# Cross attention: three rotating two-bank units in PSUM, one side bank, and one reduction for two maxima

## The reference, cut to what matters

```
q = split_heads(layernorm(x) @ w_q.T + b_q)      # (4, 16, 256, 16)
k = split_heads(ctx @ w_k.T + b_k)               # (4, 16, 4096, 16)
v = split_heads(ctx @ w_v.T + b_v)
weights = softmax(einsum('bhqd,bhkd->bhqk', q, k) / 4)
x = x + merge_heads(einsum('bhqk,bhkd->bhqd', weights, v)) @ w_o.T + b_o
```

## Time and profile before

| what | us |
|---|---|
| median of 3 runs | 4542.27 (4541.48 to 4546.44) |
| span of the profiled execution (its own time is not given apart from this) | 4533.8 |
| first cross attention: first maximum to last reduction of a maximum | 41.3 to 1019.2 |
| second: first maximum to last reduction of a maximum | 3071.3 to 4037.3 |
| TensorE, VectorE, ScalarE busy over the span | 4131.4, 3154.7, 2854.8 |

### The profile page before, as it was taken

The page is one execution under the profiler, slowest core; times in us unless marked ns, Lnnn a source line. Parts: engine busy times, 40 slices in busy tenths (PEclk is TensorE's granted clock), DMA queues, the critical chain, the costliest instruction groups (busy, mean ns, idle before and its releaser), DMA issues. The chain is left out here.

```text
span 4533.8 us, 83813 instructions
## 1 busy us (share of the span) xinstructions
PE 4131.4 (91%) x30832; PEld 2952.2 (65%) x30832; DVE 3154.7 (70%) x7414; ACT 2854.8 (63%) x5769; POOL 1819.9 (40%) x1862
## 2 busy tenths in 40 slices
PE   6999999988988999999999999977999999986898
PEld 4555555555757788887888878864555555544787
DVE  5677777776777667666676676645677777767645
ACT  3666666667866776767767777733666666664322
POOL 3222222213557555555555555523222222201544
PEclk8999999999999999999999999998999999998999
DMA  6655655535020001011010111017556655522265
GB/s 152 137 108 101 111 99 110 95 62 209 1 75 5 26 21 44 15 38 33 27 33 14 37 33 34 16 37 141 118 103 113 113 107 109 91 45 69 79 177 187
DMA packets 208206, 354.18 MB, mean 78 GB/s; under 512 B 26927, under 2 KB 110564, under 8 KB 205745
## 3 DMA queue, kind: packets, MB, share of 16 engines
q1 hardware_dynamic: 200217, 338.42, 33.5%
q0 software_dynamic: 7584, 10.39, 0.7%
HBM read 257.48 MB, written 114.98 MB: 82 GB/s over the span
## 5 line engine op out<-in xcount | busy, mean ns | idle before, releaser
L757 DVE TENSOR_REDUCE xa_m_part<-xa_ring 128x1 f32<-128x512 f32 x2048 | 1319.2, 686 | 503.5 <-PE xa_ring L910 489.0
L679 ACT ACTIVATE xa_ex<-xa_sc 128x1024 f32<-128x1024 f32 x1024 | 991.6, 1022 | 124.4 <-PE xa_sc L896 109.7
L910 PE MATMUL xa_ring<-xa_ks,xa_q_base 48*128 48x512 f32 x2048 | 521.5, 500 | 169.7 <-DVE xa_m_part L757 130.1
L1077 POOL TENSOR_SCALAR lt_p<-lt_p,lt_stat 128x192 f32<-128x192 f32 x384 | 360.4, 939 | 507.4 <-DVE lt_stat L1067 507.1
L924 PE MATMUL xa_pv<-xa_ex,xa_vs 128*17 128x256 f32 x8192 | 553.4, 388 | 1.1 <-issue 1.1
L910 PEld LDWEIGHTS xa_ring<-xa_ks,xa_q_base 48*128 48x128 f32 x2048 | 202.7, 186 | 500.4 <-DVE xa_m_part L757 431.8
L1090 ACT ACTIVATE lt_p<-lt_bank,lt_stat,lt_rq 128x128 f32<-128x128 f32 (+1 forms) x768 | 365.7, 480 | 218.9 <-DVE lt_stat L1060 214.5
L1929 PE MATMUL lt_bank<-lt_wp,lt_xt 128*128 128x512 f32 x1728 | 461.9, 409 | 16.0 <-DVE lt_wp L1766 7.1
L896 PE MATMUL xa_sc<-xa_q_base,xa_ks 50*128 50x256 f32 x4096 | 424.5, 303 | 27.7 <-ACT xa_k L659 4.1
L896 PEld LDWEIGHTS xa_sc<-xa_q_base,xa_ks 50*128 50x128 f32 x4096 | 349.4, 189 | 121.2 <-ACT xa_vs L666 24.4
L1929 PEld LDWEIGHTS lt_bank<-lt_wp,lt_xt 128*128 128x128 f32 x1728 | 314.6, 192 | 79.3 <-DVE lt_xt L1759 8.4
(11 more groups left out here) (332 smaller groups left out, 8166.4 us busy)
## 6 DMA issues: line engine op xcount, KB each, us to landing
xa_ks<-keys SPq DMA_DIRECT2D x372, 256.0 KB
keys<-xa_kp SPq DMA_DIRECT2D x128, 512.0 KB, 3.8
xa_cx<-in_ctx_t SPq DMA_DIRECT2D x64, 512.0 KB
lt_u<-in_lt_wqkv SPq DMA_DIRECT2D x54, 256.0 KB
places<-in_moe_blank SPq DMA_DIRECT2D x47, 258.0 KB, 8.7
moe_xs<-places SPq DMA_DIRECT2D x47, 258.0 KB
lt_w<-in_lt_w SPq DMA_DIRECT2D x6, 1536.0 KB
xa_q_base<-xa_m_rows SPq DMA_DIRECT2D x512, 2.0 KB
```

What stands on the lines that cost most here:

```text
L679: act.activation(x.ex[:, n % x.NE, :, :], x.sc[n % 2][:, :, :], ACT.Exp).then_inc(*x.ex_done.one())
L757: dve.tensor_reduce(x.m_part[:, i % 2, qt, h, ch:ch + 1], x.bank(n + odd), AX.X, ALU.max).then_inc(*x.dve_out.one())
L910: pe.matmul(x.bank(n + odd), x.q_base[rows, pair, b * S + qt * P:b * S + (qt + 1) * P], x.ks[unit % x.NU][rows, pair % 4, ch * 512:(ch + 1 ...
L1077: pool.tensor_scalar(sv, sv, self.stat[:, n % 5, 3, 1:2], None, ALU.mult).then_inc(*self.div_pool.one())
```

## The change: what it does

- PSUM is divided anew: three units of two banks, one bank for `pv`, one bank called `side`.
- Maxima and scores take the units in turn (S, M, S, M, ...). With three units a use waits for the use three before, which is always of the other kind: S(n) waits for R(n-2), and M(n) for E(n-1).
- The two heads of a maximum fill the two banks of a unit and signal once; one reduction makes two maxima (128x2 out of 128x1024 where there were two of 128x1 out of 128x512).
- All side work of the main loop has the one side bank, so each side step waits until the one before it has been taken away. Before the first maximum, key and query projections rotate through the side bank and the two banks of the last unit.
- The order within a turn is S, M, W, W, S, M, then `place_max`, then side work. Jobs move from 0 and 4 to 2 and 6; `max_rows` stays at 0 and `gather` at 4. Queries, `turn_out` and `project_out` keep their turns, which are at 2 and 6 of a quad as well, and stand behind the job.
- The wait of the first maxima for the turned input (`xt_dve`, `xt_act`) moves from the side step to the maximum.

```diff
-            self.ring = [ps(f"ring{i}", [P, 512]) for i in range(self.NW)]
-            self.pv = ps("pv", [P, S])
-            self.sc = [ps(f"sc{i}", [P, 4, S]) for i in range(2)]
+            self.units = [ps(f"unit{i}", [P, 2, 512]) for i in range(self.UNITS)]
+            self.pv, self.side = ps("pv", [P, 512]), ps("side", [P, 512])
...
-            if t < 0 or at % 4 == 0:
+            if at in (2, 6) or t < 0:
                 job = next(jobs, None)
...
-            scores = [("scores", n) for n in (t, t + 1) if 0 <= n < total]
-            first, second = ([("max", top)], [("max", top + 1)]) if top < total else ([], [])
-            out += first + side + second + scores if side else first + scores + second
-            if second and top % 8 == 6:
+            for odd in range(2):
+                if 0 <= t + odd < total:
+                    out.append(("scores", t + odd))
+                if top < total:
+                    out.append(("max", top + odd))
+                if odd == 0:
+                    out += [("weigh", n) for n in (t - 2, t - 1) if 0 <= n < total]
+            if top < total and top % 8 == 6:
                 out.append(("place_max", top // 8))
-            for n in (t - 2, t - 1):
-                if 0 <= n < total:
-                    out.append(("weigh", n))
+            out += side
...
+        first = [("side", self.side)] + [(f"{n}", self.units[2][:, n, :]) for n in range(2)]
...
+            if kind in ("max", "scores"):
+                n = unit % self.UNITS
+                names, place = [f"{2 * n - 4}", f"{2 * n - 3}"], self.units[n]
+                unit += 1
+            elif kind in ("key", "query") and not started:
+                name, place = first[early % 3]
+                names, early = [name], early + 1
+            elif kind in ("key", "value", "query", "gather", "max_rows", "turn_out", "project_out"):
+                names, place = ["side"], self.side
...
+            self.place_of[step] = place
+            self.before[step] = [done[n] for n in names if n in done]
+            for n in names:
+                done[n] = self.away[step]
...
-                for odd in range(2):
-                    on.wait_ge(x.full, n + odd + 1)
-                    h = 2 * pair + odd
-                    dve.tensor_reduce(x.m_part[:, i % 2, qt, h, ch:ch + 1], x.bank(n + odd), AX.X,
-                                      ALU.max).then_inc(*x.dve_out.one())
+                on.wait_ge(x.full, n + 1)
+                dve.tensor_reduce(x.m_part[:, i % 2, qt, 2 * pair:2 * pair + 2, ch:ch + 1],
+                                  x.place_of[step][:, :, :], AX.X, ALU.max).then_inc(*x.dve_out.one())
...
-            if step in x.use:
-                n = x.use[step]
-                bank = x.bank(n)
-                for m in ((n, n + 1) if kind == "max" else (n,)):
-                    if x.before[m] is not None:
-                        on.wait_ge(*x.before[m])
-            if step in x.exps:
-                on.wait_ge(x.ex_done, x.exps[step])
-                on.wait_ge(x.xt_dve, NT // 4)
-                on.wait_ge(x.xt_act, NT // 4)
+            if step in x.place_of:
+                bank = x.place_of[step]
+                for gone in x.before[step]:
+                    on.wait_ge(*gone)
```

More of the change, by code:

```diff
@@ L316, in __init__ @@
             "p (w k n) -> p w k n", w=2, k=KC)
-        self.banks = [self.sc[i // 2][:, 2 * (i % 2):2 * (i % 2) + 2, :].rearrange("p j s -> p (j s)")
-                      for i in range(4)]
+        self.banks = [self.units[i // 2][:, i % 2, :] for i in range(4)]
         f, d = c.flow, c.dma_flow
@@ L386, in steps @@
                             side.append(("ctx", m + 2))
+            if at == 0 and 0 <= quad + 1 < 4 * self.ITEMS:
+                side.append(("max_rows", quad + 1))
+            if at == 4 and 1 <= quad <= 4 * self.ITEMS:
+                side.append(("gather", quad - 1))
             b, at_b = divmod(t - 10, 12)
@@ L415, in count_uses @@
     def count_uses(self):
-        self.use, self.bank_of, self.away, self.before = {}, [], [], []
-        self.exps, self.cleared, self.chunk = {}, {}, {}
+        self.use, self.place_of, self.away, self.before, self.chunk = {}, {}, {}, {}, {}
         count = {"dve": 0, "act": 0}
-        last, ring, side, done = {}, 0, 0, [0, 0]
+        done, unit, side, early = {}, 0, 0, 0
         started = False
+        first = [("side", self.side)] + [(f"{n}", self.units[2][:, n, :]) for n in range(2)]
         for step in self.plan:
@@ L427, in count_uses @@
             started = started or kind == "max"
[L428 to L431, removed]
             if kind in ("key", "query"):
                 self.chunk[step] = len(self.chunk)
-            if kind not in ("key", "value", "query", "max", "gather", "max_rows", "turn_out", "project_out"):
-                continue
-            self.use[step] = len(self.away)
@@ L437, in count_uses @@
[L437 to L446, removed]
-                count[engine] += 1
[L448 to L451, removed]
@@ new lines, in count_uses @@
+            if kind != "scores":
+                engine = "dve" if kind in ("max", "project_out") else "act"
+                count[engine] += 1
+                self.away[step] = (self.dve_out if engine == "dve" else self.act_out, count[engine])
+                self.use[step] = len(self.use)
+            else:
+                self.away[step] = (self.ex_done, step[1] + 1)
+            self.place_of[step] = place
+            self.before[step] = [done[n] for n in names if n in done]
+            for n in names:
+                done[n] = self.away[step]
@@ L564, in sp @@
                 b = i // x.NKB
-                on.wait_ge(*x.away[x.use[step]])
+                on.wait_ge(*x.away[step])
                 if i:
@@ L629, in act @@
             if step in x.use and kind not in ("max", "project_out"):
-                n = x.use[step]
-                bank = x.bank(n)
+                n, bank = x.use[step], x.place_of[step]
             if kind == "weights":
@@ L909, in pe @@
                     rows = slice(64 * odd, 64 * odd + x.ROWS)
-                    pe.matmul(x.bank(n + odd),
-                              x.q_base[rows, pair, b * S + qt * P:b * S + (qt + 1) * P],
-                              x.ks[unit % x.NU][rows, pair % 4, ch * 512:(ch + 1) * 512],
-                              start=True, stop=True).then_inc(*x.full.one())
+                    mm = pe.matmul(bank[:, odd, :],
+                                   x.q_base[rows, pair, b * S + qt * P:b * S + (qt + 1) * P],
+                                   x.ks[unit % x.NU][rows, pair % 4, ch * 512:(ch + 1) * 512],
+                                   start=True, stop=True)
+                mm.then_inc(*x.full.one())
             elif kind == "weigh":
@@ L919, in pe @@
                 on.wait_ge(x.pv_zero, 1)
-                on.wait_ge(*x.away[x.use["value", i, kt // 2]])
+                on.wait_ge(*x.away["value", i, kt // 2])
                 if kt == 0:
@@ L953, in pe @@
                 b, = a
-                on.wait_ge(*x.away[x.use["turn_out", b]])
+                on.wait_ge(*x.away["turn_out", b])
                 on.wait_ge(x.late_in, 2 if x.ins["bv"] is None else 3)
```

31 lines of the change are left out of this document (14 added, 17 removed).

## The result

The changed kernel takes **4648.28 us** (median of 4 runs, 4636.82 to 4653.14) where the kernel before took 4541.88 beside it (4540.15 to 4546.44): ratio **1.0228, 95% interval 1.0212 to 1.0244**. It is slower by 106 us. The forecast was 4494, faster.

A forecast was written before the change was run, and what follows sets the result against it. TensorE was taken to set the pace, losing waits of about 0.3 us. Per cross attention 42 + 6 - 11 - 18 + 5 = 24 less, 48 in both: 4542.3 - 48 = 4494 us, 8-in-10 range 4400 to 4545.

The forecast's parts named there:

- The failed step: Main loop: SP's row copies move to a turn's end, keys come one turn later of six or so: 0.
- The reduction: VectorE's double reduction of 1024 elements takes 1.19 us; worth nothing by itself, as VectorE doesn't set the pace.
- The rule on smaller instructions: Skill's advice against the double reduction: by it TensorE waits up to 0.5 more, eight times, 4 us a quad.
- The plain quad: Main loop quad without combine: 13.78 in place of 14.50, 0.72 less; 42 us less in a cross attention.
- Combine: Five quads with combine steps: 8 in place of 10.1 over plain ones, three times; 6 less per cross attention.
- The exponential in the last block: A batch's last block: ScalarE's exponential waits for VectorE; 1.15 each, 16 times, 18 more per cross attention.
- The start: Before the main loop: 1.0 less in each of 9 jobs, taken as 5 less per cross attention.
- Rival 3: Main loop: TensorE's pauses for ScalarE drop the clock; slower, 4616 at one quad in 12; chance 0.06.
- Rival 2: Main loop: E late by 0.15 more each turn, 0.6 of 0.72 a quad lost; 4540 or so; chance 0.09.
- The tests that I set: Forecast wrong if a plain quad stays above 14.3, S waits for R, or mid-stretch clock falls below 0.95.

The follow-up runs named there:

- Experiment 1: Also written e1: the changed kernel with SP's load of a unit's keys (`stack_k`) ahead of the turn's side work; 4501.43 us, ratio 0.9988 to the kernel before.
- 2: The kernel before with `stack_k` one turn later, where a job stands in front of it in SP's queue; 4595.33 us, ratio 1.0210.
- experiment 4: Also written e4: Experiment 1's kernel with two reductions of 512 in a unit in place of one of 1024; 4503.78 us, ratio 0.9995 to the kernel before.
- experiment 7: Experiment 1's kernel with the exponential between blocks two turns later, behind the copy of `max_rows`; 4505.50 us, ratio 0.9920 to the kernel before.
- e8s: Experiment 1's kernel with the combine in three parts, `turn_out` and `project_out` four slots later, exponential behind `max_rows`; 4433.67 us, ratio 0.9775 to the kernel before.

## Why the prediction was wrong, point by point

- **The failed step** is "SP's row copies move from a turn's middle to its end [...]; the jobs' keys come one turn later of the six or so they have in hand: 0". I counted the lead in turns and put no price on what must fit into it. `stack_k` stood in the turn at 2, where the jobs came to be, and behind them on an in-order queue. The lead fell from 20.5 to 13.8 us and the load needs 15.75: 102 us of waits for keys, and the clock behind them. The trace of before shows the issue, the first reader and, by the share of the DMA engines, an end of the transfer near 228, some 14 us after the issue. So of the six turns in hand (a turn is 3.6 us) the load itself took more than four, and the step needed that price, not a zero. Experiment 1 takes the loss away, 2 makes it in the old kernel.
- **The reduction** was right in size (1.22) and in worth (0, experiment 4). The rule on smaller instructions would have had 4 us a quad in it; e4 and e1 lie within each other's intervals.
- **The plain quad** was right: 13.78 forecast, 13.9 measured wherever nothing else is late. Per plain quad 0.55 was gained of the 0.72 forecast (eight of before are 115.1, of e1 110.7).
- **Combine** was wrong in sign. I took 8 over five plain quads in place of 10.1. In e1 the five are 87.7, so 18.2 over five plain ones of 13.9; before they are 82.3, 9.8 over five of 14.5. I listed VectorE's instructions and not what GpSimd does in the same turn once jobs stand there. The forecast for the five was 5 x 13.78 + 8 + 2 x 0.92 for `turn_out` and `project_out` = 78.7, so 9.0 are missing at each of three places, 27 in a cross attention. That is more than the 19 to 22 missing in e1 altogether; other stretches gave some back (the last batch of the first cross attention takes 235.6 in e1 and 244.8 before, where TensorE stood 2.39 and 3.38 for nothing that the profile shows).
- **The exponential in the last block** was mis-sized: 1.15 forecast, 0.8 measured (14.7 against 13.9), once for each of the quads that experiment 7 shortens. So this term was too dear, and the miss is not here.
- **The start** was right for the turns themselves (a job 2.3 to 2.4 after the other, 3.42 before). The third key load isn't there in time, the maximum at 73.13 waited 10.60 for it, and even so the first scores start 4 us earlier than before (77.1 against 81.1), where 5 was forecast.
- **The clock.** Rival 3 had the sign and came near the size (4616), but for the wrong reason, so that was luck. TensorE's waits for ScalarE cost no clock: in e8s the weight load of a maximum waits for it 110 times in 800 us, 37.3 us in all and 0.9 at most, at a granted clock of 0.99. What cost clock were longer pauses, for a DMA or for R behind a combine. In the changed kernel, from 200 to 1000 us, 18 of TensorE's pauses took 1.89 us or more, and by single microseconds the granted clock goes to 0.50 (the 1.2 GHz level) at or soon after every one. Of the ten from 1.0 to 1.5 us it does so after six. So a late transfer costs more than its wait: in the table's batch behind the combines, waits of 1.5 to 2.7 us go with quads that are 2.6 to 4.9 longer.
- **Rival 2** has a wrong sum: a change of -11 in each of two cross attentions gives 4564 and not 4540. The reason for not expecting it stands without that number.
- The tests that I set did find it: a clock below 0.95 in a mid stretch and S waiting for R (59.6 us of S's weight loads from 200 to 1000 us). A wait for a DMA was not among them.

## What to carry to other kernels

When work moves to another turn, follow each in-order DMA queue with a price: when the issue now comes, what the instructions ahead of it on the queue wait for, how long the transfer takes to land, and when the first reader stands there. When VectorE work and GpSimd work come into the same turn, look for VectorE's operations with two inputs: they may wait for GpSimd's whole instruction. Give a new layout its own schedule before judging it: the same units of PSUM gave 1.0228, 0.9988 and 0.9775 with other orders of the side work.

## What the runs showed of the hardware

- A two-input VectorE operation with a duration of 0.29 lasts up to 2.02 when GpSimd subtracts beside it, and ends 0.15 behind it. Reductions in the same stretch keep their 1.16 and 1.22. The Trainium skill, "SBUF — State Buffer", section Who interferes with whom, says that an instruction of VectorE with two inputs in SBUF contends with one of GpSimd that reads SBUF, and that the port pair which they share is an exclusive lock; the traces agree, with 2.02 beside a subtraction of 2.36. I had not used it in the prediction. The change itself freed another such place, L768: 0.47 on average in before (0.99 at 248.91, beside a subtraction of GpSimd that ends with it), 0.17 always after. This wasn't in my sum either.
- Six loads of 256 KB, issued in 3.0 us, released their reader 15.75 us after the first issue. The write of 512 KB issued 0.47 ahead of them shares the DMA engines, which are full throughout: 375 GB/s in the microsecond where the write begins, and 98 to 156 GB/s from 230 to 240, where the loads are what is left.
- The kernel before has a median of 4506 to 4543 between groups of runs, while the 95% intervals of the ratios within a group are 0.1 to 0.3% either way: absolute times of different groups are not to be compared.
